# State space heads on one core: squares summed on VectorE, one product with ones per group, output products one head later, and turns written out with constants

## The reference

```python
proj = x @ in_proj_w.T
gate, hbc, dt = jnp.split(proj, [I, I + CD], axis=-1)
hbc = silu(causal_conv4(hbc) + conv_b)               # hs, B, C
...
# for each head: Y[l] = sum over s <= l of (C_l . B_s) exp(A_cum[l] - A_cum[s]) X_s, X = hs * dt
y = (Y_diag + Y_off).reshape(b, s, H, P) + D_res      # D_res = D * hs
h32 = y * jax.nn.silu(gate)
g = h32.reshape(b, s, I // gs, gs)                    # a group: 4 heads, 512 columns
var = jnp.mean(g * g, axis=-1, keepdims=True)
h32 = (g * jax.lax.rsqrt(var + EPS)).reshape(b, s, I)
return norm_w * h32 @ out_proj_w.T
```

## Time and profile before

| what | value |
|---|---|
| time, median of 3 runs | 3301.8 us |
| lowest and highest | 3299.2 us and 3311.94 us |
| span of the profiled execution | 3378.8 us |
| PE, DVE, ACT, POOL busy over that span | 78%, 54%, 45%, 36% |
| the heads, first half: from the block's start to its last add | 140.67 to 662.96 us |
| the heads, second half | 758.0 to 1280.6 us |

### The profile page before, as it was taken

One profiled execution on the slowest core, in us unless ns is written; L12 is line 12 of the kernel. 1 busy time (PEld: TensorE's weight loads), 2 busy tenths in 40 slices (PEclk: granted clock), 3 DMA queues, 4 the chain that ended last, 5 costly groups with the idle time before them and its releaser, 6 DMA issues. The chain is left out here.

```text
span 3378.8 us, 47321 instructions
## 1 busy us (share of the span) xinstructions
PE 2632.3 (78%) x13662; PEld 1672.9 (50%) x13663; DVE 1810.1 (54%) x3839; ACT 1526.6 (45%) x2976; POOL 1228.9 (36%) x1164
## 2 busy tenths in 40 slices
PE   5799999888999994777759558885578335988984
PEld 2467777655777773444435323332445112555652
DVE  4666676585666665888851367773222501222334
ACT  3555555464555550888951136663255100223321
POOL 1477777536777771000000100000000172244443
PEclk8999999999999996666659769997689656899997
DMA  2121121003112101900000000000000051477875
GB/s 63 47 57 26 56 57 33 13 7 88 34 49 57 38 13 62 340 1 1 1 30 0 17 1 1 1 1 4 18 1 0 26 181 49 93 165 171 179 172 125
DMA packets 127073, 192.73 MB, mean 57 GB/s; under 512 B 17552, under 2 KB 88208, under 8 KB 125584
## 3 DMA queue, kind: packets, MB, share of 16 engines
q1 hardware_dynamic: 83696, 134.71, 14.1%
q0 software_dynamic: 23616, 33.24, 5.6%
q10 hardware_dynamic: 19584, 22.57, 2.4%
HBM read 123.23 MB, written 67.25 MB: 56 GB/s over the span
## 5 line engine op out<-in xcount | busy, mean ns | idle before, releaser
L228 DVE SCALAR_TENSOR_TENSOR h_pre<-h_px,h_par,h_pre 128x510 f32<-128x510 f32 (+2 forms) x384 | 286.4, 746 | 268.7 <-ACT h_pre L689 248.9
L652 PE MATMUL h_po<-h_wo,h_h 128*128 128x256 f32 x1024 | 328.2, 411 | 0.0
L2890 POOL DMA_INDIRECT moe_sums<-ex_y,ex_sidx x132 | 204.9, 1553 | 314.9 <-DVE ex_y L3058 296.7
L574 POOL TENSOR_SCALAR h_decay<-h_cumb,h_sel 128x256 f32<-128x256 f32 x256 | 292.4, 1142 | 25.2 <-DMA h_cumb<-cum_rows 25.2
L585 POOL TENSOR_TENSOR h_mix<-h_decay,cb 128x768 f32<-128x768 f32 x128 | 232.6, 1817 | 164.3 <-ACT h_decay L675 164.3
L616 PE MATMUL h_px<-x_cols,h_w 128*128 128x512 f32 x512 | 254.4, 620 | 25.3 <-DMA h_d<-d_skip 25.3
L843 POOL TENSOR_TENSOR norm_rstd<-norm_mv,mhalf 128x4 f32<-128x4 f32 x24 | 28.3, 1178 | 605.0 <-DVE norm_mv L826 605.0
L621 PE MATMUL h_pz<-x_cols,h_w 128*128 128x512 f32 x512 | 242.8, 597 | 5.6 <-DVE h_gate L742 5.6
L701 ACT ACTIVATE h_xt<-h_pxt,h_sel 128x128 f32<-128x128 f32 x512 | 146.0, 368 | 152.1 <-PE h_pxt L640 152.1
L2935 PE MATMUL ex_pg<-ex_w,ex_xT 128*128 x528 | 196.1, 495 | 21.8 <-ACT ex_xT L2993 6.2
L654 PEld LDWEIGHTS h_pss<-ones,h_sq 128*128 128x128 f32 x1024 | 194.6, 190 | 26.3
(11 more groups left out here) (389 smaller groups left out, 5823.6 us busy)
## 6 DMA issues: line engine op xcount, KB each, us to landing
h_cumb<-cum_rows SPq DMA_DIRECT2D x32, 1024.0 KB, 8.5
moe_tiles<-blank SPq DMA_DIRECT2D x4, 6642.0 KB, 44.2
ex_w<-moe_w SPq DMA_DIRECT2D x64, 352.0 KB
ex_xg<-moe_tiles ACTq DMA_DIRECT2D x136, 162.0 KB
ex_wd<-moe_wd SPq DMA_DIRECT2D x64, 176.0 KB
h_w<-w_xg SPq DMA_DIRECT2D x8, 1024.0 KB, 10.4
moe_sums<-blank SPq DMA_DIRECT2D x2, 2176.0 KB, 26.7
h_wo<-w_out SPq DMA_DIRECT2D x8, 512.0 KB, 10.2
```

Of the source, the lines that this page charges most:

```text
L228: ins = dve.scalar_tensor_tensor(out=out[:, :, back:S], in0=src[:, :, 0:S - back], scalar=par[:, at + CK - 1 - back:at + CK - back], in1=o ...
L574: pool.tensor_scalar(decay[j][:, u, 0:S], cumb[s.vb][:, j, u, :], sel[s.vb][:, u * TPB, 1, j:j + 1], 0.0, ALU.subtract, ALU.min)
L652: pe.matmul(po[t // TPB][:, t % TPB, :], hh[j % 2][:, t * P:(t + 1) * P], w_out[s.pg][:, j, :], start=(j == 0 and t % TPB == 0), stop=(j = ...
L2890: pool.indirect_dma_start(out=r.sums[i % 2][:, :], out_offset=bass.IndirectOffsetOnAxis(ap=sidx[i][:, 0:1], axis=0), in_=y[i % 2][:], in_o ...
```

## The change

The changed lines all lie in `mamba_heads`, with `Step` and the functions that write the turns out.

1. **Squares.** ACT squares the first head of a step into a new tile sqs (two of them, by the step's parity) and the three others into sq. DVE adds each of those three into sqs (`total`, 128x512, one head later). PE multiplies sqs with the column of ones once per step, four products behind the last head's output products, instead of four per head; `variance` waits for that (`pooled`).
2. **Output products one head later.** PE's turn k does `out` of k-1 instead of k. h has four buffers instead of two, and `out` no longer waits for the square.
3. **Variance, root and add.** With it, `variance` and `add` of the step before stand in a step's second turn, j == 1, `variance` ahead of `conv` and `open_`, `add` behind them. `root` on POOL stands between the two halves of the first `argue` of a step.
4. **Turns written out.** All steps are written out with constants in place of loops with registers; the LEAD drains, DVE's clearing of po and pss, and the dummy `variance`, `root` and `add` ahead of the first step fall away, and SP's first load waits for nothing.

```diff
         def out(s, j, h):
-                pe.wait_ge(finished, LEAD + h + 1)
-                pe.wait_ge(squared, LEAD + h + 1)
+                pe.wait_ge(finished, h + 1)
                 if j == 0:
-                    pe.wait_ge(added, LEAD + s.n)
-                    pe.wait_ge(scaled, LEAD + s.g + 1)
+                    after(pe, added, s.n)
+                    pe.wait_ge(scaled, s.g + 1)
                 for t in range(TW):
-                    pe.matmul(po[t // TPB][:, t % TPB, :], hh[j % 2][:, t * P:(t + 1) * P], w_out[s.pg][:, j, :],
-                              start=(j == 0 and t % TPB == 0), stop=(j == HG - 1), skip_group_check=True)
-                    mm = pe.matmul(pss[:, t:t + 1], sq[j % 2][:, t * P:(t + 1) * P], r.ones[:, 0:1],
-                                   start=(j == 0 and t == 0), stop=(j == HG - 1), skip_group_check=True)
+                    mm = pe.matmul(po[t // TPB][:, t % TPB, :], hh[j][:, t * P:(t + 1) * P], w_out[s.pg][:, j, :],
+                                   start=(j == 0 and t % TPB == 0), stop=(j == HG - 1), skip_group_check=True)
                 mm.then_inc(outed, 1)
+                if j == HG - 1:
+                    pe.wait_ge(totalled, (s.n + 1) * (HG - 1))
+                    after(pe, vared, s.n)
+                    for t in range(TW):
+                        mm = pe.matmul(pss[:, t:t + 1], sqs[s.vb][:, t * P:(t + 1) * P], r.ones[:, 0:1], start=True, stop=True)
+                    mm.then_inc(pooled, 1)
-            parts = ((3, project), (1, scan), (2, turn), (0, out))
+            parts = ((3, project), (1, scan), (2, turn), (-1, out))
...
             def square(s, j, h):
+                act.wait_ge(finished, h + 1)
+                if j == 0:
+                    after(act, pooled, s.n - 1)
+                    act.activation(sqs[s.vb][:], hh[j][:], ACT.Square).then_inc(squared, 1)
+                else:
+                    after(act, totalled, s.n * (HG - 1) + (0, 0, -1, 1)[j])
+                    act.activation(sq[j % 2][:], hh[j][:], ACT.Square).then_inc(squared, 1)
...
+            def total(s, j, h):
+                if j:
+                    dve.wait_ge(squared, h + 1)
+                    dve.tensor_tensor(sqs[s.vb][:], sqs[s.vb][:], sq[j % 2][:], ALU.add).then_inc(totalled, 1)
...
             def argue(s, j, h):
                 for u in range(2):
+                    if u == 1 and j == 0 and s.n >= 2:
+                        root(STEPS[s.n - 2])
...
-            def body(prev, cur, nxt):
-                for j in range(HG):
-                    finish(*head(cur, nxt, j))
-                    if j == 0:
-                        variance(prev)
-                    slot(((2, silu),), cur, nxt, j)
-                    if j == 0:
-                        if nxt:
-                            select(nxt)
-                        add(prev)
-                    slot(((3, conv), (3, open_)), cur, nxt, j)
+            def body(k):
+                n, j = divmod(k, HG)
+                if n == len(STEPS):
+                    dve.drain()
+                slot(((0, finish), (-1, total), (2, silu)), k)
+                if j == 0 and n + 1 < len(STEPS):
+                    select(STEPS[n + 1])
+                if j == 1 and n >= 1:
+                    variance(STEPS[n - 1])
+                slot(((3, conv), (3, open_)), k)
+                if j == 1 and n >= 1:
+                    add(STEPS[n - 1])
```

More of the change, by code:

```diff
@@ L54, in __init__, with after @@
         self.spent = []
+def after(eng, sem, count):
+    if count > 0:
+        eng.wait_ge(sem, count)
 def clear(nc, sems):
@@ L408, with __init__, head_slots, at_head @@
 class Step:
-    def __init__(self, g2, pg, two, vb):
-        self.g2, self.pg, self.vb, self.two = g2, pg, vb, two
-        self.g = g2 * 2 + pg
-        self.p = two * 2 + vb
-        self.n = self.g * NP + self.p
-        self.opens = isinstance(two, int) and self.p == 0
-def head_turns(eng, body, group=None):
-    def groups(g2, last):
-        for pg in range(2):
-            if group:
-                group(g2, pg)
-            before = Step(g2, 0, NP // 2 - 1, 1) if pg else Step(g2 - 1, 1, NP // 2 - 1, 1)
-            after = Step(g2, 1, 0, 0) if pg == 0 else (None if last else Step(g2 + 1, 0, 0, 0))
-            body(before, Step(g2, pg, 0, 0), Step(g2, pg, 0, 1))
-            with eng.Fori(0, NP // 2 - 1) as i:
-                body(Step(g2, pg, i, 0), Step(g2, pg, i, 1), Step(g2, pg, i + 1, 0))
-                body(Step(g2, pg, i, 1), Step(g2, pg, i + 1, 0), Step(g2, pg, i + 1, 1))
-            body(Step(g2, pg, NP // 2 - 1, 0), Step(g2, pg, NP // 2 - 1, 1), after)
-    with eng.Fori(0, GH // 2 - 1) as g2:
-        groups(g2, False)
-    groups(GH // 2 - 1, True)
+    def __init__(self, n):
+        self.n = n
+        self.g, self.p = divmod(n, NP)
+        self.g2, self.pg = divmod(self.g, 2)
+        self.two, self.vb = divmod(self.p, 2)
+STEPS = [Step(n) for n in range(GH * NP)]
+def head_slots(first, last, body):
+    for k in range(first, len(STEPS) * HG + last):
+        body(k)
+def at_head(h):
+    return (STEPS[h // HG], h % HG, h) if 0 <= h < len(STEPS) * HG else None
 def mamba_heads(nc, a, r, half, cum_rows, dtc, cb):
@@ L516, in mamba_heads, with slot, group @@
         block = ctx2.enter_context(nc.Block())
-        def head(cur, nxt, j):
-            step, j = (cur, j) if j < HG else (nxt, j - HG)
-            return (step, j, step.n * HG + j) if step and j >= 0 else None
-        def slot(parts, cur, nxt, j):
+        def slot(parts, k):
             for ahead, part in parts:
-                at = head(cur, nxt, j + ahead)
-                if at:
-                    part(*at)
+                if at_head(k + ahead):
+                    part(*at_head(k + ahead))
         @block.sync
         def _(sp):
-            def group(g2, pg):
-                sp.wait_ge(added, LEAD + (g2 * 2 + pg - 1) * NP)
-                g = (g2 * 2 + pg) * 2 + half
+            def group(s):
+                pg = s.pg
+                after(sp, added, (s.g - 1) * NP)
+                g = s.g * 2 + half
                 sp.dma_start(w_in[pg][:], a["w_xg"][g]).then_inc(loaded[pg], 16)
@@ L541, in cum, with group @@
             def cum(s):
-                sp.wait_ge(argued, LEAD + (s.n - 1) * HG)
+                after(sp, argued, (s.n - 1) * HG)
                 sp.dma_start(cumb[s.vb][:].rearrange("p j u l -> p j (u l)"),
                              cum_rows[bass.ds((s.g * 2 + half) * HG, HG), bass.ds(s.p * 2 * S, 2 * S)].partition_broadcast(P)).then_inc(cums[s.vb], 16)
-            with sp.Fori(0, GH // 2) as g2:
-                for pg in range(2):
-                    group(g2, pg)
-                    with sp.Fori(0, NP // 2) as two:
-                        for vb in range(2):
-                            cum(Step(g2, pg, two, vb))
-            sp.wait_ge(added, LEAD + GH * NP)
+            for s in STEPS:
+                if s.p == 0:
+                    group(s)
+                cum(s)
+            sp.wait_ge(added, len(STEPS))
         @block.gpsimd
         def _(pool):
-            for one in (scaled, matched, argued):
-                pool.drain().then_inc(one, LEAD)
             pool.memset(halves[:], 0.5)
             pool.drain()
-            pool.drain().then_inc(rooted, LEAD - 1)
-            def group(g2, pg):
-                pool.wait_ge(loaded[pg], (g2 + 1) * 64)
+            def group(s):
+                pg = s.pg
+                pool.wait_ge(loaded[pg], (s.g2 + 1) * 64)
                 pool.tensor_tensor(dskip[pg][:], dskip[pg][:], halves[:], ALU.mult)
```

138 lines of the change are left out of this document (54 added, 84 removed).

## The result

The changed kernel takes **3322.2 us** (median of 12 runs), the kernel before in the same comparison 3308.3 (12 runs). The ratio is 1.0045, with a 95% interval of 1.003 to 1.0061: 10 to 20 us **slower**. The forecast was 3289 us in a range of 3274 to 3316, so the time lies above the range. Of the 33 us between them, 6.5 lie in where the sum started: from 3301.8, the median of three runs, where the twelve give 3308.3. The profiled execution spans 3322.5 us and agrees with the timed runs.

The account below looks back on a forecast made before the run. PE was taken to bound the heads, 7.80 us per head. The terms -86.4 - 3.4 + 63.3 + 7.0 + 3.0 + 3.4 gave -13.1 us, from 3301.8 to 3289 us, range 3274 to 3316.

Parts of the forecast that it names:

- what the squares cost and what stays: PE's products with ones: 0.90 us per head, three of four go, 86.4 us saved; the four left cost 0.9 to 1.1.
- the wait for the adds: In a step's second turn PE waits 2.26 us for DVE's adds behind the gate, 28 times: 63.3 us.
- The last step's wait: In each half's last step PE waits about 3.5 us for root and adds, twice: 7.0 us.
- the start: SP's first load no longer waits 1.7 us for the drains on DVE: 3.4 us saved over both halves.
- the tail: The last head's output products come one turn later, the same work in PE's row: priced at nothing.
- the group starts, 0.5 us each: POOL's scaling of w_out makes mix, root and adds up to 0.5 us late at six places: 3.0 us.
- rival 2: The root is late: POOL's mix or argue 1 us later lengthens each wait by about 0.55, 3304 us; chance 0.15.
- priced at nothing, by that cover: DVE's three added adds of squares, 2.1 us per step, fit its idle time before the taps, 1.1 us slack left.
- the clock, 3.4 us: PE's granted clock falls only behind the two long waits of 3.5 us, 1.7 us each: 3.4 us.
- rival 3: The clock falls with each of 28 waits, 48 us more, 3337 us; one in three, 3305; chance 0.10.

Follow-up runs that it names:

- run 1: Changed kernel with variance and adds into x put back ahead of the taps and the root at the turn's start, ahead of the mix: 3269.1 us.
- run 5: Changed kernel with four more TensorE products, results unused, just ahead of the wait for the adds: 3300.6 us.
- run 12: Changed kernel, adds still behind the gate, with y written over py and the tanh over px in PSUM: 3290.6 us.
- run 10: Changed kernel with adds into x ahead of the taps, and y and ScalarE's tanh written into PSUM (py and px): 3225.6 us.
- run 3: Changed kernel with GpSimd's scaling of the next group's output weights three turns earlier: 3305.3 us.

## Why the prediction was wrong

- **Right: what the squares cost and what stays.** Turns of 6.90; the eight instructions with ones add 0.81 (7.72 against 6.91), a little under the 0.9 to 1.1.
- **Right: the wait for the adds.** Place, cause and size: 2.04 to 2.19 of idle (once 2.39), 9.27 to 9.4 for the turn, where the steps of the sum give 9.2. Run 1 confirms it by taking it away. The last step's wait was 2.87 with the root behind the last mix, forecast 3.5; the root takes 1.03 here and not 1.40, since no xs runs beside it (see the last section).
- **Right: the start**, 140.70 for SP's first load against 142.44, and the tail: the last adds end 24.79 us behind the last px, before 22.04, of which 2.87 are that wait.
- **Wrong: the group starts, 0.5 us each.** They cost 3.3 to 3.5, 20.6 us in all instead of 3.0. The step that failed is rival 2's: I read from the earlier trace rows that DVE and POOL only drag on each other, 0.98 instead of 0.69. That row stands beside an argue. Started inside a mix, the same kind of instruction takes up to 2.35. The prediction had the rule of a full wait before it, and took the milder row for the case. What the 0.5 also left out is that PE's wait, once longer, brings a fall of the clock: by run 5 about 1.7 of a group start's cost.
- **Wrong by the same step: "priced at nothing, by that cover"**. The totals were priced by their own 0.69. They also move xs by 0.6 us into the mix, and then it costs 1.6 more. In the changed kernel most of that stays in the slack behind PE's wait, so it shows at the group starts and in the first steps only; with the wait gone (run 1) it is the bound, 40 us.
- **Wrong: the clock, 3.4 us.** Nine falls at waits and two in the ramps; run 5 prices the nine at 15 to 18 us. The term is 3.4, and its size failed as well as its place. I put them at the two longest waits, and there (2.87) no fall came. They came at all eight waits that had grown to 2.9 us or more in front of a step's first output products, and once (472 us) behind one of 2.2; rival 3's "one in three" was close in number, 9 of 28, but eight of the nine follow the longest waits. In run 12, with ordinary waits alone, 4 of 28 brought one.

So the forecast's sum was that of a kernel in which the meetings of DVE and POOL cost PE nothing, and such a kernel, run 12, is 31.6 us under the changed one. From 180 to 640 us in the timelines: in the kernel before, none of 119 xs and h starts inside a mix. 15 xs start 0.51 to 0.53 ahead of one and still run when it begins, and that mix takes 1.83 or 1.84 and not 1.81. In the changed kernel 31 of 161 xs, h and totals do, with a median of 2.30 us. So the trace of before could not show the price. But the 15 show that the margin was 0.5 us, under one instruction of DVE, and the change adds one ahead of xs.

The Trainium skill (SBUF — State Buffer, "Who interferes with whom") states the rule that I weighed and set aside: a VectorE instruction with two SBUF inputs contends with a GpSimd instruction that reads SBUF, and one with at most one SBUF input, outside the 2-port modes, does not. Runs 10 and 12 agree with it, 682 ns against 1624 in the mean of xs; for an argue the traces show something milder than a full block.

## What to carry to other kernels

Before a VectorE instruction is added, moved or shifted in time, look up which of VectorE's instructions read two operands from SBUF and where GpSimd's long two-operand instructions stand: such a pair cost the rest of GpSimd's instruction and 0.55 us here, not a few tenths, and the instruction that pays is often the neighbour of the one that was added. Where an operand has just been in PSUM, leave it there; written over a buffer that is read by then, it cost no time here and no room. And an idle stretch of TensorE that is under 1 us longer than its neighbours (2.93 against 2.04) can cost a clock fall of 1.7 us on top: price waits that lie close to one that has shown it.

## What the runs showed of the hardware

- DVE instructions with two inputs of 128x512 in SBUF take 0.69 us alone and a median of 2.30 when they start inside a mix (both inputs in SBUF, 1.81). In all 56 such cases of the changed kernel's heads they end 0.55 us behind the mix (one 0.56), so the later into it they start, the less they take (1.46 at 0.90 into it). A mix that begins while such an instruction runs can end late in its turn, up to 2.36 long in that kernel. Inside an argue (one tensor input) they take 0.68 to 0.88, and it is the argue that grows: 1.13 alone, 1.57 with one such instruction, 2.10 with two or three.
- With one input in PSUM the same DVE instruction beside the same mix takes 0.68 or 0.69 (20 of 20 from 180 to 640 us in run 12); the totals there, still with two, take 0.84 to 2.06.
- Small copies are caught too, though each has one input. A step's four copies of 128x8 take 0.39 us in all in the kernel before. In the changed one 17 of 32 such groups start inside a mix, and all 17 take 2.2; the same in run 3, where the mix had started 0.30 ahead of them:

```profile
296.44 2.23 DVE L704 COPY h_sel<-dtc 128x8 f32<-128x8 f32 x4
...
296.14 2.05 POOL L580 TENSOR_TENSOR h_mix<-h_decay,cb 128x768 f32<-128x768 f32 x1 [1.03 <-ACT h_decay L660]
```

- POOL pays as well. Its root of 128x4 takes 1.40 us in all 32 cases of the kernel before, and in 30 of run 1, in which an xs had started 0.17 us ahead of it; with none beside it, 1.01 to 1.04. In run 10 the xs stands at the same place, but reads one input from PSUM, and the root takes 1.03 in all 30. The xs ahead of the root of the earlier trace rows, which starts at 610.15, and the pair in run 10:

```profile
609.98 0.68 DVE L748 SCALAR_TENSOR_TENSOR h_xs<-h_tx,h_pre 128x512 f32<-128x512 f32 x1
```

```profile
235.31 0.68 DVE L717 SCALAR_TENSOR_TENSOR h_xs<-h_px,h_pre 128x512 f32<-128x512 f32 x1
...
235.48 1.03 POOL L581 TENSOR_TENSOR h_rstd<-h_var,mhalf 128x4 f32<-128x4 f32 x1 [1.65 <-DVE h_var L739]
```

  So the 1.40 of the earlier trace rows already held 0.37 us of the two engines' meeting.
- Idle stretches of PE of 2.04 to 2.40 us left the granted clock at 2.4 GHz in 24 of 28 cases of run 12. In the changed kernel the eight of 2.93 to 3.17 were followed by 3.4 us at 1.2 GHz, the 2.87 at each half's end by none. In run 1, two of the six stretches of 2.11 at group starts were, and in the ramps 3.58 was (the kernel before) and 3.50 was not (run 12). What decides between these stays open.
